# Gate and up of 1024 tokens as a 2x2 block product formed with seven block products instead of eight; activations go through DRAM

## What is computed

```python
    x = x + _L0_cond_ref(x, L0_cond_weights, itok_B_0_15)          # out[b] = W[cond[b]]^T x[b], 64x64
    x = x + _L1_cond_ref(x, ...)
    x = x + _L2_cond_ref(x, ...)                                    # causal convolution per row, masked
    x = x + _L3_cond_ref(x, itok_B_0_31, ...)                       # as the first, with a bias
...
        gate = lora_add(jnp.einsum('bnh,fh->bnf', x, W_gate), x, A_gate, B_gate)
        up = lora_add(jnp.einsum('bnh,fh->bnf', x, W_up), x, A_up, B_up)
        act = jax.nn.silu(gate) * up
        down = lora_add(jnp.einsum('bnf,hf->bnh', act, W_down), act, A_down, B_down)
```

## Time and profile before

| what | value |
|---|---|
| device time, median of 3 runs | 1831.37 us (1830.07 to 1832.57) |
| span of the profiled execution | 1830.0 us |
| PE busy | 1795.7 us, 98% of the span, 9336 matmuls |
| DVE busy | 841.9 us, 46% |
| ACT busy | 534.5 us, 29% |
| POOL busy | 182.8 us, 10% |
| mean granted PE clock | 0.996 of full speed |
| moved by DMA | 261.98 MB, 143 GB/s on the mean |

### The profile page before, as it was taken

How to read it: one execution, slowest core, us unless ns; L and a number is a source line. 1 busy time by engine, 2 the same in 40 slices (tenths; PEclk the granted TensorE clock), 3 DMA queues, 4 the chain that set the end, 5 groups by cost and what they waited for, 6 DMA issues and landing times.

```text
span 1830.0 us, 27921 instructions
## 1 busy us (share of the span) xinstructions
PE 1795.7 (98%) x9336; PEld 1540.6 (84%) x9336; DVE 841.9 (46%) x1074; ACT 534.5 (29%) x646; POOL 182.8 (10%) x311
## 2 busy tenths in 40 slices
PE   5999999999999999999999999999999999999998
PEld 5888888888888888888888888888888888879997
DVE  3867433334344334334433344335434344328887
ACT  2342222112222222112222222113222222126665
POOL 4400442000000000000000000003400000003230
PEclk8999999999999999999999999999999999999999
DMA  6533777432333335333333335333333336346764
GB/s 211 161 101 120 259 257 236 149 120 93 113 103 113 115 106 172 124 115 104 106 115 114 103 113 175 120 109 112 119 113 104 115 110 210 104 157 237 240 195 184
DMA packets 124096, 261.98 MB, mean 143 GB/s; under 512 B 27046, under 2 KB 62342, under 8 KB 123686
## 3 DMA queue, kind: packets, MB, share of 16 engines
q1 hardware_dynamic: 108726, 231.46, 38.9%
q0 software_dynamic: 10992, 23.31, 3.9%
q10 hardware_dynamic: 4352, 6.88, 1.0%
HBM read 246.61 MB, written 38.57 MB: 156 GB/s over the span
## 4 chain that ended last, share of the span: by engine, by line
PE 95%; DVE 2%; issue 1%; DMA 1%; POOLq 0%; ACT 0%; POOL 0%; SPq 0%; DVEq 0%
PE ps L731 77%; PE ps L779 5%; PE ps L883 5%; PE ps L880 3%; PE ps L912 1%; PE ps L755 1%; PE ps L813 1%; PE ps L816 1%; PE ps L841 1%; PE ps L897 1%; DMA bgu_of_batches<-in_bgu 0%; DVE wlo L1131 0%; DVE u_hl L1309 0%; DMA raw<-bgu_of_batches 0%; PE ps L741 0%
## 5 line engine op out<-in xcount | busy, mean ns | idle before, releaser
L731 PE MATMUL ps<-xhi,whi 128*128 128x512 f32 (+1 forms) x1440 | 559.4, 388 | 10.0 <-DVE wlo L1131 9.3
L731 PE MATMUL ps<-xlo,whi 128*128 128x512 f32 (+1 forms) x1440 | 557.7, 387 | 0.0
L731 PE MATMUL ps<-xhi,wlo 128*128 128x512 f32 (+1 forms) x1440 | 555.7, 386 | 0.0
L1236 DVE TENSOR_TENSOR wlo<-raw,whi 128x1280 fp32r<-128x1280 f32 x160 | 239.9, 1500 | 292.4 <-ACT whi L637 292.2
L731 PEld LDWEIGHTS ps<-xhi,whi 128*128 128x128 f32 x1440 | 272.8, 189 | 61.2 <-issue 7.7
L731 PEld LDWEIGHTS ps<-xhi,wlo 128*128 128x128 f32 x1440 | 272.2, 189 | 55.4
L637 ACT ACTIVATE whi<-raw 128x1280 fp32r<-128x1280 f32 x168 | 214.1, 1274 | 350.1 <-PE ps L779 327.6
L731 PEld LDWEIGHTS ps<-xlo,whi 128*128 128x128 f32 x1440 | 272.9, 190 | 47.3
L731 PE MATMUL ps<-act_hi,whi 128*128 128x512 f32 x672 | 262.5, 391 | 0.0
L731 PE MATMUL ps<-act_lo,whi 128*128 128x512 f32 x672 | 262.2, 390 | 0.0
L731 PE MATMUL ps<-act_hi,wlo 128*128 128x512 f32 x672 | 261.8, 390 | 0.0
(11 more groups left out here) (188 smaller groups left out, 1623.1 us busy)
## 6 DMA issues: line engine op xcount, KB each, us to landing
raw<-in_wgu SPq DMA_DIRECT2D x172, 512.0 KB, 3.3
rtoep<-k_dram SPq DMA_DIRECT2D x64, 512.0 KB, 4.4
raw<-in_wd SPq DMA_DIRECT2D x96, 256.0 KB, 2.9
raw<-bgu_of_batches SPq DMA_DIRECT2D x336, 64.0 KB, 2.9
raw<-in_wd SPq DMA_DIRECT2D x32, 640.0 KB, 3.8
bgu_of_batches<-in_bgu POOLq DMA_DIRECT2D x30, 352.0 KB, 4.2
xn<-in_x SPq DMA_DIRECT2D x16, 512.0 KB, 6.1
out<-ostage SPq DMA_DIRECT2D x16, 512.0 KB, 2.6
```

The costliest lines, as they stand in the source:

```text
L731: ins = pe.matmul(bank, wt[:, w, k, :], r(k), start=start and k == first and n == 0, stop=stop and k == first + nblk - 1 and n == 2)
L1236: tt(wlo[:, g, 0:KB + 2, :], raw[:, g, 0:KB + 2, :], f32(whi[:, g, 0:KB + 2, :]), ALU.subtract).then_inc(lo_done[g], 1)
```

## The change

All four chunks are handled in two passes (`pass_(p)`, p = 0 and 1) of two chunks each, 1024 tokens. In a pass the 21 full blocks of features become 21 frames. In `frame(p, f)` the gate and up blocks of 128 features for both chunks are one product of 2x2 blocks: the rows are gate and up, the inner dimension is the two halves of h, and the columns are the two chunks. It is formed with seven block products of 4 x 3 matmuls of 512 columns (`Q1, Q6, Q5, Q7, Q2, Q3, Q4`), whose operands are sums and differences of weight blocks and of token blocks. Eight block products made it before.

- Token operands: `form_hi`, `form_lo` and `t1_raw` to `t4_raw` make seven operands with high and low part (`xop`), once per pass.
- Weight operands: SP loads the four blocks of a frame (`raw`, one buffer each, 256 KB each); DVE forms the three sums and one difference (`sums`), ACT makes the high parts (`a_split`), DVE the low parts (`a_low`).
- Results: DVE combines the banks of PSUM in seven additions and multiplications (`u2, t5, u3, g1`), ACT takes silu, both split the result (`act_split`, `act_low`), and ACT stores the activations to DRAM (`act_dram`).
- Units and `rest` of the second chunk: the second chunk's first half of h no longer exists as an operand, only as Q1 + Q5, so its products there take twice the matmuls (`x_parts`).
- Down: SP loads one weight tile of all 1024 outputs (512 KB) and one activation tile (256 KB) per step of 128 features; all eight banks add up over 21 steps (`down_step`). The LoRA B of down comes in two steps in between, and the arithmetic of the convolution's rows (`step_exponents_and_angles` to `sum_of_u`) stands between the down steps of the second pass, where it stood between width blocks before.
- First layer: the weights of the first pass are in `wbd_a`. Those of the second are gathered into `wbd_b`, which lies over the buffer of the weight sums (`asum`), and go to DRAM (`w0_dram`) and back.

Core of the diff, new code:

```diff
+        (asum,), ev_base = place(sum_base, [("asum", [P, 3, KH, P], F32)])
+        (wbd_b,), _ = place(sum_base + KH * P * 4, [("wbd_b", [P, NQ, P], F32)])
...
+        @block.sync
...
+            def loads_of(p, f, group=None):
...
+                sp.wait_ge(lb_lo, lb_before)
+                load_lb(p, f)
+                sp.wait_ge(a_sum, sums_a11)
+                sp.wait_ge(a_lo, lo_a11)
+                load_block(f, A11)
+                sp.wait_ge(a_lo, lo_a21)
+                load_block(f, A21)
+                sp.wait_ge(a_lo, lo_a12)
+                sp.wait_ge(a_sum, sums_before)
+                load_block(f, A12)
+                sp.wait_ge(a_lo, lo_before)
+                load_block(f, A22)
...
         @block.gpsimd
...
+            with pool.Fori(0, NQ) as n:
+                gather_w(wbd_a, n, n, 0, 0, w0, w0_in[0])
+            for c in range(2):
+                for half in range(2):
+                    with pool.Fori(0, HB) as b:
+                        gather_bgu(0, c, half, b, lora_key(0, c, half, b), NF, FB, bgu_rest_in)
...
+            for c in range(2):
+                for half in range(2):
+                    with pool.Fori(0, HB) as b:
+                        gather_bgu(0, c, half, b, lora_key(0, c, half, b), 0, 1, bgu_in)
+            for c in range(2):
+                for half in range(2):
+                    with pool.Fori(0, HB) as b:
+                        gather_ad(0, c, half, b, lora_key(0, c, half, b))
+            for f0, f1 in ((1, NF // 2), (NF // 2, NF)):
+                for c in range(2):
+                    for half in range(2):
+                        with pool.Fori(0, HB) as b:
+                            gather_bgu(0, c, half, b, lora_key(0, c, half, b), f0, f1, bgu_in)
+            with pool.Fori(0, NQ) as n:
+                for g in range(2):
+                    gather_w(wbd_b, n, NQ + n, g, 0, w0, w0_in[2])
+            pool.wait_ge(w0_in[2], 16 * 2 * NQ)
+            add_identity(wbd_b, NQ).then_inc(w0b_ready, 1)
+            pool.wait_ge(w0b_ready, 1)
+            pool.dma_start(w0_dram[:, :, :], wbd_b[:, :, :]).then_inc(w0_stored, 16)
...
         @block.scalar
...
+            def frame(p, f, grp, last):
...
+                a_split(p, f, Q4)
+                act.wait_ge(lb_in, 32 * n_f(p, f + 1, 1))
+                copy(lb_hl[:, 0, :, :], lb_raw[:, :, :]).then_inc(lb_hi, 1)
+                act.wait_ge(prod, n + 1)
+                reach(act, ev, n_ev(p, f) - 4)
+                copy(u2[:, :], ps[:, BA, :]).then_inc(p1_copied, 1)
+                if not last:
+                    a_split(p, f + 1, Q1)
...
+                act_split(p, f, 1, 6)
+                act_split(p, f, 0, 8)
...
         @block.tensor
...
+            def x_parts(c, kh):
+
+                return ((Q1,), (Q2,))[kh] if c == 0 else ((Q1, Q5), (Q3,))[kh]
...
+            def frame(p, f):
...
+                pe.wait_ge(ev, e + 2)
+                product(p, f, Q3, BC, False)
+                lora_b(ps[:, BC, :], lb_hl, 1, 0).then_inc(prod, 1)
+                pe.wait_ge(ev, e + 3)
+                lora_b(ps[:, BE, :], lb_hl, 1, 1).then_inc(prod, 1)
...
+                product(p, f, Q4, BB, True)
+                lora_b(ps[:, BB, :], lb_hl, 0, 1).then_inc(prod, 1)
...
         @block.vector
...
+            def sums(p, f):
...
+                dve.wait_ge(raw_in[A21], landed)
+                dve.wait_ge(raw_in[A22], landed)
+                tt(s1, a21, a22, ALU.add).then_inc(a_sum, 1)
...
+            def frame(p, f, j, last):
...
+                a_low(p, f, Q4)
+                dve.wait_ge(lb_hi, n_f(p, f + 1, 1))
+                tt(lb_hl[:, 1, :, :], lb_raw[:, :, :], f32(lb_hl[:, 0, :, :]), ALU.subtract).then_inc(lb_lo, 1)
+                if not last:
+                    a_low(p, f + 1, Q1)
...
+                tt(u2[:, :], ps[:, BB, :], u2[:, :], ALU.add).then_inc(ev, 1)
+                if not last:
+                    sums(p, f + 1)
...
+                tt(t5[:, :], ps[:, BC, :], u2[:, :], ALU.add).then_inc(ev, 1)
...
+                act_low(p, f, 1, t5, 1)
+                dve.wait_ge(prod, n + 8)
+                tt(u3[:, :], ps[:, BB, :], u3[:, :], ALU.add).then_inc(ev, 1)
+                dve.wait_ge(ev, e + 7)
+                tt(u3[:, :], g0[:, :], u3[:, :], ALU.mult).then_inc(ev, 1)
+                act_low(p, f, 0, u3, 2)
...
+                for kh in range(2):
+                    unit_lo(p, 3, kh)
+                if first:
+                    dve.wait_ge(w0_stored, 16)
+                sums(p, 0)
+                if first:
+                    form_lo(p, 4)
+                    t3_raw(p)
+                t_unit(p, 2)
```

More of the change, by code:

```diff
@@ L42 @@
 KB = T // P
+KH = KB // 2
 PAIRS = B // 2
[L44 to L49, removed]
+NQ = PAIRS // NP
+NF = F // P
+REST = F - NF * P
+FB = NF + 1
 HB = CB // 2
 HT = TOK // 2
[L54 to L61, removed]
+GRP = 3
+NGRP = NF // GRP
+assert REST * 2 == P and HB * RANK * 2 == P and NGRP * GRP == NF and TOK == 512
+NPROD = 7
+Q1, Q6, Q5, Q7, Q2, Q3, Q4 = range(NPROD)
+A11, A21, A12, A22 = range(4)
+PER_F = 8
+STEPS = 24
+BD_S = 10
+REST_S = STEPS - 1
 LS = 32
@@ L142, in build @@
+        assert at <= xr_base
         s = dict(zip(small, sm))
[L144 to L147, removed]
         s |= {"dt_": ex_x[:, 0, :], "ea": ex_x[:, 1, :]}
-        (ve,), _ = place(x1out_base, [("ve", [P, C, LS], F32)])
@@ new lines, in l0 @@
+            def l0(p, q):
+                pe.wait_ge(x_in[q], 16 * (p + 1))
+                if q >= KH:
+                    pe.wait_ge(l0_copied, p * NQ + q - KH + 1)
+                b = L0_BANKS[p][q]
+                wb = (wbd_a, wbd1)[p]
+                for k in range(KB):
+                    ins = pe.matmul(ps[:, b + k // 4, (k % 4) * P:(k % 4) * P + P],
+                                    xn_of(p, q)[:, k * P:(k + 1) * P], wb[:, q, :], start=True, stop=True)
+                ins.then_inc(l0_done, 1)
@@ new lines, in _, with pass_ @@
+            pe.wait_ge(w0_ready, 1)
+            for q in range(NQ):
+                l0(0, q)
+            def pass_(p):
+                if p:
+                    pe.wait_ge(x1_done, KB + 2)
+                for u in range(2):
+                    if p == 0 and u == 0:
+                        pe.wait_ge(x_lo, 2)
+                        pe.wait_ge(l0_copied, NQ)
+                    unit(p, u)
+                if p:
+                    pe.wait_ge(x1_done, KB + 3)
+                rest(p, 0)
+                pe.wait_ge(x_lo, p * NPROD + 4)
+                unit(p, 2)
+                unit(p, 3)
+                if p:
+                    pe.wait_ge(x1_done, 2 * KB)
+                rest(p, 1)
+                frame(p, 0)
+                with pe.Fori(1, NF) as f:
+                    frame(p, f)
+                if p == 0:
+                    pe.wait_ge(w0_back, 16)
+                    l0(1, 0)
+                    pe.wait_ge(ev, n_ev(0, NF))
+                    l0(1, 1)
+                    a_down(0, NF - 1)
+                    l0(1, 2)
+                    pe.wait_ge(t_ready, 10)
+                    for q in range(3, NQ):
+                        l0(1, q)
+                else:
+                    a_down(1, NF - 1)
+                down_chunk(p, 0)
+                down_chunk(p, 1)
```

1622 lines of the change are left out of this document (1020 added, 602 removed).

## The result

The changed kernel takes 2048.8 us (median of 4 runs, 2043.1 to 2052.2) against 1832.0 for the kernel before on the same chip. The ratio is 1.118, with a 95% interval of 1.116 to 1.121. So it is slower by 217 us, inside the range on record (1910 to 2055), 70 above the predicted 1979 and outside 1950 to 2010, the range that the main case had for itself. The profiled execution spans 2050.3 us.

A forecast was written before the change was run, and what follows sets the result against it. PE's matmuls bound the kernel before; after the change each frame waits on a 23.2 us loop through other queues. Matmuls alone give 1727 us; 252 more (about 140 start, 55 frames, the rest seams) make 1979, range 1910 to 2055.

The forecast's parts named there:

- the main case: Whole kernel: frame loop, late start and seams as summed, 1979 us, own range 1950 to 2010; chance 0.50.
- the rival with the clock: PE before Q3: clock falls at each wait, 1.7 us more per frame, 2050 us in all; chance 0.12.
- The loop: Each frame, through PE, DVE, ACT and SP: 23.2 us (22.4 to 24.2); PE needs 21.9 and waits 1.3 before Q3.
- the landing of the six loads: In each frame, SP's loads behind `lb_lo`, 1.57 MB: landed after 6.7 us, bounds 5.9 to 7.6.
- The 10 us that I had added for POOL's gathers: First three frames: POOL's 64 gathers of the second pass slow their loads, 10 us (0 to 25).
- The late start: Before frame 0: DVE's sums wait for POOL's gather list and the `wbd_b` store until 187 us (175 to 205).
- The seams: Between frames and down chunks: 23 us after pass 0's frames, 42 at pass 1's front, 12 after its frames.
- the 14 that I let stick out: Second pass's down chunks: of 55 us of DVE's convolution-row work, some 14 stick out beyond the steps.
- POOL's list is short: At the start: 0.6 us a gather, store at 80, 107 us less, 1872 us; chance 0.08.
- DMA is cheap: Start and frames: gathers 0.52 us a DMA, loads 2.9 us a set, 1799 us, faster by 32; chance 0.04.
- Loads land sooner: In the frames: loads land at the issue limit or sooner, PE sets 21.9 us a frame, 1924 us; chance 0.17.
- the 1727 of PE alone: Whole kernel: span if nothing else waited, 1830.0 less 103.3 us of matmuls saved, 1726.7 us.

The follow-up runs named there:

- experiment 1: Changed kernel with SP issuing the next frame's four weight blocks first and the LoRA B loads with their `lb_lo` wait last: 1933.8 us.
- 6: Changed kernel with Q1's twelve matmuls issued twice per frame, an eighth product: 2060.3 us.
- 11: Changed kernel with DVE making the second result `t` ahead of the four sums instead of behind them: 2002.6 us.
- 7: Changed kernel loading only the first chunk's half of LoRA B from frame 1 on, 0.26 MB less per frame, same issues: 2017.8 us.
- 8: Changed kernel loading only the first half of each weight block's rows from frame 1 on, 0.52 MB less per frame, same issues: 1985.2 us.
- 9: Changed kernel with a frame's four block loads as one DMA of 1 MB, still behind `lb_lo`: 2183.0 us.
- experiment 3: Changed kernel with the two 2 MB stores of the first down chunk split into eight of 0.5 MB behind the step loads: 2037.2 us.
- experiment 2: Changed kernel with SP gathering `wbd_b` and half the `ad` tiles instead of POOL, and frame 1's wait split: 1956.9 us.
- experiment 5: Changed kernel with SP's order, start and store burst repaired, then POOL's LoRA B gathers in one set and SP's gathers in idle stretches: 1815.6 us.

## Why the prediction was right in kind and 70 us short

- **What bounds.** Right. The frames lost an eighth of their large matmuls and the time went up, because each frame waits for another queue.
- **The range.** 2048.8 is 6 us inside the upper bound and outside the main case's own range. It is within 2 us of the rival with the clock (2050), and that is chance: the rival's mechanism explains 15 us of the 70.
- **The loop.** Its route was right at each station: behind Q3's start, `g` began at 3.5 (3.6 predicted), `u` was made at 9.0 (9.25), `lb_lo` stood at 12.9 (13.2), and the sums and `t` took 3.2 (3.3). Experiments 1, 6 and 11 show the loop from three sides.
- **The failed step is the landing of the six loads**: 6.7 us taken, with bounds of 5.9 to 7.6; measured 8.6 in the frame shown and 8.2 in the median. I had 2.2 us of latency and the bytes at 352 GB/s, which makes 4.5 us for them. The window over the burst shows share and rate:

```profile
1415.00:1416.00 1.00, 1.00 (x6) 0.84 (x5) 0.00 (x0) 0.00 (x0) 0.00 (x0) 1.00 0.00 0
...
1416.50:1423.20 6.70, 6.70 (x35) 5.68 (x34) 1.29 (x2) 0.63 (x1) 0.00 (x0) 1.00 0.82 233
```

  Hardly anything moves until 1.5 us after `lb_lo`, and then the 1.57 MB take 6.7 us. So the latency was about right, and the time of the bytes was 2.2 us too short. By the first of the earlier trace rows a share of 0.82 would go with 290 GB/s, by the second with 254; it was 233. The marginal bytes of 7 and 8 cost no more than at full rate and the issues of 9 cost nothing, so what keeps the burst under its rate stays open. By the Trainium skill ("DMA: Bandwidth & Descriptors", Anatomy of one DMA), which gives its 2.0 us and 436 GB/s for one DMA issued by GpSimd, 1.57 MB would take 5.6 us, an estimate; for six loads of SP behind one wait the trace does not agree (8.2).
- **What the sum made of it.** From Q3 to Q3 are 24.7 us in the second pass, 1.5 more than the 23.2 of the sum and outside its bounds of 22.4 to 24.2. The landing explains 1.5, the clock 0.4, and the other stations take 0.3 off. The 10 us that I had added for POOL's gathers in the first frames hid a part of this miss in the first pass: its frames were no further apart than those of the second, and only its first stands out (11.4 from `lb_lo` to the sum).
- **The clock.** I gave its rival 0.12, as "each wait". In fact the waits came out at 1.2 to 2.8 us, not 1.3, and ten of 40 took the clock down: 15 us, on the loop. The price of 1.7 that I had was near (1.3 to 1.6, but for the longest wait). Experiment 9 is that rival in full: waits of 2.9 to 7.4 us, a fall in each. The Trainium skill ("TensorE: Matmul & The Clock Gate", HAM oscillation) describes such a loop, and there the trace agrees (40 falls behind 40 waits).
- **The late start.** Right in place and cause, and 9 us short: POOL's 16 keys with two DMAs took 40.1 us (36.3 taken), one of them 4.5, and a LoRA B gather up to 1.65, some of them 2.2 (1.58). Frame 0 itself took 6 more, in good part by a wait of 8.7 and the clock.
- **A term was missing**: the two stores of 2 MB behind the LoRA B of down. 10.85 us of PE, and 11.6 of time in experiment 3. They stand in SP's list ahead of the next step's loads, and I had followed that list in the frames alone.
- **The seams** (units, rests, transition, row arithmetic between down steps, end) were right to 1 us each, in sum. Inside the second pass's down chunks one term was worked out wrong: 34 and 13 us of the convolution's rows make 47, not 55, and the 14 that I let stick out follows from neither; PE's waits for `act_hl` there are 9.0 us.
- **The rivals.** "POOL's list is short" and "DMA is cheap" had been priced as if the queues ran at their issue cost; neither was seen. "Loads land sooner" was wrong in its sign. Of the 324 us by which the span lies over the 1727 of PE alone, 125 were the start's wait, about 115 the frames' loop (experiment 1) and 12 the burst; the other 72 were not taken apart by a run.

## What to carry to other kernels

Before an arithmetic saving is counted, follow one buffer round its loop through every in-order queue: here one wait for a small tile at the head of SP's list held four large loads that had been free for long, and cost the whole gain. A wait that PE shows is the last link only; turning the order round at that link moved it (46 us), and removing its cause took it away (115). Put bulk stores behind the loads that the next step needs, and count gathers by key as a queue with a price of its own.

## What the runs showed of the hardware that was not expected

- Six loads, 1.57 MB in all, behind one wait landed 8.6 us after it in one frame, at 233 GB/s, and 7.6 to 9.0 us passed until the first sum in 38. One DMA in place of four did not land sooner (8.9 us), although the last issue was 1.8 us earlier.
- The clock fell in 8 of 19 waits between 1.99 and 2.77 us and in none of 19 up to 1.94, in one run. In the runs of experiments 8 and 9 it fell once at 1.93 and at all 40 from 2.89 up. Yet in experiment 2's run it fell behind 1.94 us and stayed up behind 2.82, 2.93 and 3.07. So the length of the wait alone did not decide it:

```profile
1415.74 3.01 PE L1088 MATMUL ps<-xop,aop_b 128*128 128x512 f32 x12 [3.07 <-DVE t L1703]
1439.91 4.21 PE L1088 MATMUL ps<-xop,aop_b 128*128 128x512 f32 x12 [1.94 <-DVE t L1703]
```

- Keyed gathers of one DMA cost mostly 1.4 to 1.7 us each on POOL and 1.2 to 1.5 on SP (in experiment 5 eight of `wbd_b` in 9.74 and eight in 11.76 us), so that moving them to SP gained by the second queue, hardly by a cheaper one.
